# A joined graph kernel: one PSUM bank in four is emptied by VectorE in the SAGE stages, lists are loaded a step further ahead, and the node phase writes the first table itself

## The reference

```python
x = _layernorm(x + _L0_gnn_ref(x, ...))          # attention; its LayerNorm is the "node phase" below
def _sage_conv(x, src, dst, Wl, Wr, b):
    agg = segment_sum(x[src], dst) / maximum(cnt, 1)[:, None]
    return agg @ Wl.T + x @ Wr.T + b
h = relu(_bn_eval(_sage_conv(x, ...), ...))
h = _bn_eval(_sage_conv(h, ...), ...)
x = _layernorm(x + h)
```

## Time and profile before

| what | us |
|---|---|
| median of 3 runs | 10389.19 |
| lowest, highest | 10364.29, 10482.84 |
| the profiled execution | 10510.41 |
| its span in the trace | 10508.6 |
| TensorE, VectorE, ScalarE, POOL recorded busy | 6286.0, 4845.1, 3259.5, 5222.7 |
| mean granted TensorE clock | 0.667 |

### The profile page before, as it was taken

One profiled execution on the slowest core, in us unless ns is written; L12 is line 12 of the kernel. 1 busy time (PEld: TensorE's weight loads), 2 busy tenths in 40 slices (PEclk: granted clock), 3 DMA queues, 4 the chain that ended last, 5 costly groups with the idle time before them and its releaser, 6 DMA issues.

```text
span 10508.6 us, 188490 instructions
## 1 busy us (share of the span) xinstructions
PE 6286.0 (60%) x45410; PEld 4168.3 (40%) x45411; DVE 4845.1 (46%) x14741; ACT 3259.5 (31%) x7648; POOL 5222.7 (50%) x4883
## 2 busy tenths in 40 slices
PE   2255555455555754444444444446399999599999
PEld 2143434344343543444444444434244444244444
DVE  4344444444445315555555555541155555344454
ACT  0001010010102004333333444442155555355555
POOL 1365655556551005555555555514366666466665
PEclk9866666666666555555555555555599998788898
DMA  2322222122223332222122122212244433333333
GB/s 81 31 44 56 44 57 43 43 57 44 56 43 90 114 52 37 36 37 36 36 36 36 36 36 37 37 19 61 70 104 105 104 104 103 89 98 95 98 101 90
DMA packets 742656, 655.51 MB, mean 62 GB/s; under 512 B 455893, under 2 KB 635506, under 8 KB 742253
## 3 DMA queue, kind: packets, MB, share of 16 engines
q0 software_dynamic: 194624, 386.92, 17.2%
q1 hardware_dynamic: 476344, 244.24, 9.0%
q10 hardware_dynamic: 71640, 23.81, 0.9%
HBM read 570.87 MB, written 83.23 MB: 62 GB/s over the span
## 4 chain that ended last, share of the span: by engine, by line
PE 32%; issue 20%; another core or an unknown queue 14%; DVE 13%; DVEq 6%; ACT 5%; DMA 4%; SPq 3%; POOL 2%; ACTq 1%; POOLq 0%
PE psc L1387 10%; PE psa L1370 9%; PE psc L1257 2%; PE psa L1524 2%; PE psa L1296 2%; SPq L855 2%; ACT oht L1018 1%; ACT acc L1124 1%; DVEq L529 1%; ACT ohb L1015 1%; PE psc L1284 1%; DMA t_gat<-acc 1%; PE psc L1358 1%; PE psc L1360 1%
## 5 line engine op out<-in xcount | busy, mean ns | idle before, releaser
L552 POOL DMA_INDIRECT rows<-t_gat,idx x3200 | 3156.4, 986 | 2897.7 <-PE psa L1296 1149.7
L573 POOL DMA_INDIRECT acc<-t_part,acc x1400 | 1793.8, 1281 | 1036.4 <-issue 791.8
L1124 ACT ACTIVATE acc<-psa 128x384 bf16<-128x384 f32 x3200 | 1443.7, 497 | 1429.7 <-PE psa L1370 1163.4
L1296 PE MATMUL psa<-rhs,rows 128*128 128x176 f32 (+1 forms) x6400 | 1719.8, 422 | 152.2 <-issue 119.1
L1296 PEld LDWEIGHTS psa<-rhs,rows 128*128 128x128 f32 x6400 | 1492.7, 307 | 208.2 <-issue 177.3
L1370 PE MATMUL psa<-den,rhs 125*32 125x384 bf16 x12800 | 1189.6, 363 | 198.8 <-ACT acc L1124 149.3
L1018 ACT ACTIVATE oht<-psc 66x1024 bf16<-66x1024 bf16 x406 | 413.8, 1019 | 2295.2 <-remote 1912.3
L1387 PE MATMUL psc<-acc,oh_dst 128*125 128x384 bf16 x2300 | 851.1, 419 | 0.0
L1268 PE MATMUL psc<-adw,oht 66*128 66x17 bf16 (+1 forms) x3248 | 152.2, 173 | 1054.5 <-ACT oht L1018 1035.5
L1387 PE MATMUL psc<-acc,stg 128*125 128x384 bf16 x2300 | 743.4, 366 | 2.5 <-DMA acc<-t_part,acc 2.5
L1284 PE MATMUL psc<-oh,wgt 128*8 128x22 f32 (+1 forms) x6400 | 329.0, 206 | 678.7 <-issue 483.5
(11 more groups left out here) (321 smaller groups left out, 8261.2 us busy)
## 6 DMA issues: line engine op xcount, KB each, us to landing
rows<-list_src SPq DMA_DIRECT2D x200, 500.0 KB
rows<-t_gat,idx POOLq DMA_INDIRECT x3200
acc<-y_d SPq DMA_DIRECT2D x50, 1000.0 KB, 5.0
y_d<-stg SPq DMA_DIRECT2D x100, 250.0 KB, 2.0
acc<-t_part,acc POOLq DMA_INDIRECT x1400
acc<-t_sage SPq DMA_DIRECT2D x300, 62.5 KB
adw<-win_d SPq DMA_DIRECT2D x836, 2.2 KB
adw<-win_d SPq DMA_DIRECT2D x788, 0.4 KB
```

Source lines behind the costliest of these rows:

```text
L552: eng.indirect_dma_start(rows[:, j, 0:spec["width"]], None, spec["table"], bass.IndirectOffsetOnAxis(ap=idx[:, j:j + 1], axis=0)).then_inc ...
L573: eng.indirect_dma_start(h_prow[u][:, t, :], None, t_parts[layer], bass.IndirectOffsetOnAxis(ap=h_idx[u][:, t:t + 1], axis=0)).then_inc(h_ ...
L1124: eng.activation(h_rows[:, g, :], psa[:, g % 4, 0:D3], ACT.Copy).then_inc(hyb["ev"], 1)
L1296: last = eng.matmul(sums(half, q, h), rows[:, half * TH + j, 0:D], right, start=(j == 2 * q), stop=(j == 2 * q + 1))
```

## The change

In the SAGE node stages VectorE evicts the gathers 3, 7, 11 and 15, ScalarE the other twelve, with a semaphore each (`evd`, `ev`). TensorE's order becomes four segments, then four gathers, and so on. VectorE's order within a step is new. SP loads source and target list of tile t+1 in step t, where it loaded those of tile t; indices and own rows stay (`rest`, `own`). In the node phase VectorE applies factor and shift and makes the three parts, POOL only stores, and the parts of the first 16 chunks are written into `table1` in place of a buffer, so that the first layer's four loads of it go.

```diff
@@ -102,6 +102,20 @@
+def by_four_from_table(eng, in_table, *stages):
+    for lo, hi, table in ((0, in_table, True), (in_table, NC // 4, False)):
+        with eng.Fori(lo, hi) as i:
+            for first in (0, 2):
+                for stage in stages:
+                    for u in (first, first + 1):
+                        stage(i * 4, u, table)
+    for first in range(0, NC % 4, 2):
+        for stage in stages:
+            for u in range(first, min(first + 2, NC % 4)):
+                stage(NC // 4 * 4, u, False)
@@ -325,6 +339,9 @@
+        def fin_parts(e, u, table):
+            return table1[:, ds((e + u) * TC, TC), :] if table else z_parts[u % 2]
@@ -408,12 +425,11 @@
-        hyb = phase_sems("h", ("ohs", "ohd", "gps", "ev", "seg", "comb", "var", "std", "norm", "own"),
+        hyb = phase_sems("h", ("evd", "ohs", "ohd", "gps", "ev", "seg", "comb", "var", "std", "norm", "own"),
...
-        pool_l = sem("pool_l")
@@ -590,36 +606,23 @@
-        def pool_fin(eng, npl):
+        def pool_fin(eng):
...
-            def store(e, u):
-                link = DynLinks(eng, pool_l, npl)
-                z, parts = zt[:, u % 2, :, :], z_parts[u % 2]
+            def store(e, u, table):
...
-                eng.sem_inc(alone, 1)
-                eng.dma_start(rows_of(t_sage0, e + u), z).then_inc(S[f"out{u % 2}"], 16)
-                left = z
-                for r in range(3):
-                    link(eng.tensor_copy(parts[:, :, r * D:(r + 1) * D], left))
-                    eng.sem_inc(alone, 1)
-                    if r < 2:
-                        link(eng.tensor_tensor(z_rest, left, parts[:, :, r * D:(r + 1) * D], ALU.subtract))
-                        eng.sem_inc(alone, 1)
-                        left = z_rest
-                link.end()
-                eng.dma_start(rows_of(t_parts[0][AHEAD:, :], e + u), parts).then_inc(S[f"out{u % 2}"], 16)
-            def stored(e, u):
+                eng.dma_start(rows_of(t_sage0, e + u), zt[:, u % 2, :, :]).then_inc(S[f"out{u % 2}"], 16)
+                eng.dma_start(rows_of(t_parts[0][AHEAD:, :], e + u), fin_parts(e, u, table)).then_inc(S[f"out{u % 2}"], 16)
+            def stored(e, u, table):
...
-            by_four(eng, store, stored)
+            by_four_from_table(eng, KB // (4 * TC), store, stored)
-            ni, nk, fst, npl = (eng.alloc_register(f"{n}_pool") for n in ("ni", "nk", "fst", "npl"))
-            eng.reg_mov(npl, 0)
+            ni, nk, fst = (eng.alloc_register(f"{n}_pool") for n in ("ni", "nk", "fst"))
@@ -805,7 +808,10 @@
-                if before:
+            def rest(e, k):
+                u, n = k % 2, e + n0
+                if later(e, k):
@@ -819,10 +825,13 @@
             def step(e, t):
+                if there(e, t + 1):
+                    lists(e, t + 1)
...
-                    lists(e, t)
+                    rest(e, t)
...
+            lists(0, 0)
@@ -933,7 +942,7 @@
-                for k in range(0, KB, KB // 4):
+                for k in range(0, KB, KB // 4) if layer else ():
@@ -1090,13 +1099,6 @@
-            def finish(e, u):
-                eng.wait_ge(S["norm"], e + (u + 1))
-                for t in range(TC):
-                    z = zt[:, u % 2, t, :]
-                    last = eng.activation(z, z, ACT.Identity, bias=lnb[:, u % 2, t:t + 1], scale=lnr[:, u % 2, t:t + 1])
-                last.then_inc(S["row"], 1)
@@ -1105,10 +1107,10 @@
             def pair(stages, e, chunks):
-                pair([deviation, finish], i * 2, (0, 1))
+                pair([deviation], i * 2, (0, 1))
...
-            pair([deviation, finish], NC // 2 * 2 - 2, (0, 1))
-            pair([deviation, finish], NC - 1, range(NC % 2))
+            pair([deviation], NC // 2 * 2 - 2, (0, 1))
+            pair([deviation], NC - 1, range(NC % 2))
@@ -1141,11 +1143,11 @@
             def step(e, t):
-                    if gather:
+                    if gather and g % 4 < 3:
...
-                    if node and g == 5:
+                    if node and g == 7:
...
-                    if node and layer and g == 12:
+                    if node and layer and g == GP - 1:
@@ -1360,12 +1362,19 @@
+            def emptied(e, k, g):
+                k, g = (k - 1, g + GP) if g < 0 else (k, g)
+                if g % 4 == 3:
+                    eng.wait_ge(hyb["evd"], (e + n0) * 4 + (k * 4 + g // 4 + 1))
+                else:
+                    eng.wait_ge(hyb["ev"], (e + n0) * 12 + (k * 12 + g // 4 * 3 + g % 4 + 1))
             def gather(e, k, g):
-                    eng.wait_ge(hyb["ev"], n * GP + (k * GP + g - 3))
+                    emptied(e, k, g - 4)
@@ -1380,7 +1389,7 @@
-                    eng.wait_ge(hyb["ev"], n * GP + (k * GP + g + 1))
+                    emptied(e, k, g)
@@ -1389,15 +1398,17 @@
             def step(e, t):
-                for g in range(GT):
-                    if there(e, t - 1):
+                for first in range(0, GP, 4):
+                    for g in range(first, first + 4) if there(e, t - 1) else ():
...
-                    if there(e, t) and g < GP:
+                    for g in range(first, first + 4) if there(e, t) else ():
...
-                    if there(e, t - 2) and g == 4:
+                    if there(e, t - 2) and first == 4:
...
-                    if there(e, t - 2) and g == 10:
+                    if there(e, t - 2) and first == 8:
...
+                for g in range(GP, GT) if there(e, t - 1) else ():
+                    segment(e, t - 1, g)
@@ -1871,19 +1882,31 @@
+            def evict(e, k, g):
+                eng.wait_ge(hyb["gps"], (e + n0) * GP + (k * GP + g + 1))
+                eng.tensor_copy(h_rows[:, g, :], psa[:, g % 4, 0:D3]).then_inc(hyb["evd"], 1)
+
             def step(e, t):
                 if there(e, t):
-                    targets(e, t)
+                    evict(e, t, 3)
+                if there(e, t + 1):
+                    sources(e, t + 1)
+                if there(e, t):
+                    evict(e, t, 7)
                 if there(e, t - 2):
                     turned(e, t - 2)
-                if there(e, t + 1):
-                    sources(e, t + 1)
+                if there(e, t):
+                    evict(e, t, 11)
                 if there(e, t - 2):
                     centre(e, t - 2)
                     if layer:
                         scale(e, t - 2)
+                if there(e, t):
+                    evict(e, t, 15)
                 if there(e, t - 1):
                     combine(e, t - 1)
+                if there(e, t):
+                    targets(e, t)
@@ -2188,14 +2211,25 @@
-                def scale(e, u):
-                    own = Links(eng, S["own_b"], (e + u) * 2)
+                def scale(e, u, table):
+                    own = Links(eng, S["own_b"], (e + u) * 8)
...
-                    eng.sem_inc(S["norm"], 1)
-                by_four(eng, centre, scale)
+                    for t in range(TC):
+                        z = zt[:, u % 2, t, :]
+                        last = ts(z, z, lnr[:, u % 2, t:t + 1], lnb[:, u % 2, t:t + 1], ALU.mult, ALU.add)
+                    own(last)
+                    left = zt[:, u % 2, :, :]
+                    for r in range(PARTS):
+                        part_r = fin_parts(e, u, table)[:, :, r * D:(r + 1) * D]
+                        own(eng.tensor_copy(part_r, left))
+                        if r < PARTS - 1:
+                            own(tt(z_rest, left, part_r, ALU.subtract))
+                            left = z_rest
+                    eng.sem_inc(S["row"], 1)
+                by_four_from_table(eng, KB // (4 * TC), lambda e, u, table: centre(e, u), scale)
```

More of the change, by code:

```diff
@@ L688, in _ @@
             phase_end(eng, 7)
-            pool_fin(eng, npl)
+            pool_fin(eng)
             phase_end(eng, 8)
```

## The result

| kernel | median us | lowest, highest | executions |
|---|---|---|---|
| before | 10436.01 | 10364.29, 10501.15 | 4 |
| changed | 11807.43 | 11790.81, 11814.90 | 4 |

Ratio 1.131, 95% interval 1.122 to 1.141: slower, as forecast, but by 1371 us where 500 were forecast, and above the range, which ended at 11,650. The runs were made in sets, each with the kernel before beside it, and the kernel before took about 10,500 us (medians of 10,436 to 10,536) in some sets, this one among them, and about 8,900 in others, so ratios are taken inside a set, and a step is named with the set's condition, "10,500" or "8,900".

What follows compares the result with a forecast made beforehand. TensorE, not eviction, was taken to set the SAGE pace. Steps of 13.9 + 2.6 + 0.9 = 17.4 us gave +660 us, less 104 and 57: +499, so 10,890 us; range 10,200 to 11,650.

Steps and rivals of the forecast that it cites:

- The handover: SAGE step: TensorE's first segment waits for the mask, now behind `combine` on VectorE; 5.0 us a step.
- TensorE's batched step: SAGE step: TensorE's work with segments and gathers in batches, at full clock, takes 8.9 us, 2.9 less.
- The clock: SAGE step: after each stop TensorE restarts at 1.2 GHz, 5.2 us of work at half rate; +2.6 us a step.
- rival B: SAGE stages: clock stays at half through every step's work; 21.1 us a step, 11,630 us in all; chance 0.18.
- Late signals: SAGE step: VectorE waits five times for TensorE signals that come late; +0.9 us a step, bounds 0 and 2.5.
- Node phase: Node phase before SAGE: conversions moved from POOL to VectorE shorten two chunks from 28.2 to 19.9 us; -104 us.
- The table load: Before the first SAGE layer: without four loads on SP's queue, the index list and everything after come earlier; -57 us.
- A: SAGE stages: clock holds or returns at once; 13.9 to 14.0 us a step, 10,200 us in all; chance 0.15.
- C: SAGE stages: eviction is the bound and two engines halve it; step 12.0 us or below, 9810 us; chance 0.05.

Runs made afterwards that it cites:

- run 4: Changed kernel unaltered, measured again in a set where the kernel before took 8901.18 us: 9778.09 us, ratio 1.099, step 17.0 us.
- run 1: Changed kernel with only `targets(t)` moved back to the head of VectorE's step: 9183.22 us, ratio 1.030 to the kernel before.
- run 7: Kernel before with only `targets(t)` moved last in VectorE's step, behind `combine(t-1)`: 11476.47 us, ratio 1.289, step 25.0 us.
- run 6: Changed kernel with 26 extra matmuls, never read, at the end of each TensorE step: 9293.94 us, ratio 1.044, step 14.5 us.
- run 9: Beside the kernel before at 10,523 us: changed kernel unaltered, 11966.15 us; changed kernel with one of POOL's seven gathers per tile, 10972.62 us.
- run 10: Changed kernel with ScalarE emptying all 16 banks and VectorE's order of before, batches and lists kept: 8701.84 us, ratio 0.978, step 11.57 us.
- run 11: Two edits of run 10's kernel: one POOL gather per tile, 8355.09 us; target mask made by 23 small comparisons, 8531.30 us, ratio 0.958.
- run 12: Kernel before with the change's node phase, table load and lists a step ahead: 8722.24 us, ratio 0.980; in condition 10,500, 10401.41 us, ratio 0.989.

## Why the prediction was right or wrong

**The handover was right in place and near in size.** 5.0 us forecast; 5.21 in the step above, and on the mean 5.9 in the changed kernel and 5.75 in run 4, where no signal is late (total us, times, longest; the changed kernel, then run 4):

```profile
PE psc L1396 <- DVEq L1828: 1172.3, 200, 11.0
```
```profile
PE psc L1396 <- DVEq L1828: 1145.2, 199, 6.1
```

The terms of run 4, means against the forecast: `combine` begins 0.67 us behind the last segment's record (0.35; VectorE is often still evicting bank 15) and takes 1.20 with its gaps (0.95), small operation and gap 0.40 (0.42), mask 3.16 (3.15), signal 0.34 (0.1). With `targets` first the stop is gone (run 1); with it last in the kernel before it appears (run 7, 5.26).

**TensorE's batched step, 8.9 us, was right.** Run 6 shows 8.84 at full clock, and 8.84 + 5.75 + 2.4 gives the 17.0 measured without late signals.

**The clock, +2.6 us, was right:** 2.4 by run 6. That the forecast chose it over rival B was in part luck: nothing in the argument told the orders apart, the reason given was the time from rest at the layers' starts of the interleaved order, and with the handover the interleaved order went B's way (run 7).

**Late signals, +0.9 us, is the term that failed.** It was bounded at 0 to 2.5 by one lateness read in one step of the kernel before. Measured: 21.6 - 17.0 = 4.6 us between the conditions, and 4.8 by run 9. The trace of before held more than the step that was read: 228 evictions over 1 us late, up to 4.6 us, and a gather of POOL ran or had just ended in each of these delays. What it couldn't show is how much the interleaved order hid; that order loses only 1.9 us a step to the condition (14.0 against 12.05). In the changed kernel four gathers go out together, TensorE needs their banks some two microseconds later, and each stop costs clock as well. Inside a step, from the first segment to the last, TensorE takes 15.8 us on the mean where it takes 11.3 in run 4: 3.0 of the difference are stops, the other 1.5 longer busy time at the lower clock. The step is 4.2 us above the 17.4 forecast, or some 830 of the 871 us missed: late signals 3.7 more than priced and the handover 0.75 more, batches and clock 0.2 less.

**Node phase, -104 us, gave 57.** The period of two chunks fell from 28.2 to 24.2 us, forecast 19.9. The chain in the changed kernel:

```profile
7122.22 0.18 DVE L2217 RECIPROCAL lnr<-lnr 125x4 f32<-125x4 f32 x1
...
7127.07 0.18 DVE L2217 RECIPROCAL lnr<-lnr 125x4 f32<-125x4 f32 x1
...
7127.48 1.69 DVE L2222 TENSOR_SCALAR acc<-acc,lnr,lnb 125x128 f32<-125x128 f32 x4
...
7131.90 0.43 DVE L2227 CAST den<-rows 125x512 f32 x1
...
7134.47 1.32 POOL L616 DMA_DIRECT2D t_part<-den  x1
...
7143.86 0.69 DVE L2202 TENSOR_TENSOR acc<-psa,acc 125x512 f32<-125x512 f32 x1 [3.36 <-POOLq L620]
```

Scaling takes 4.9 and 5.3 us (7122.22 to 7127.07 to 7132.3) where 4.2 each was priced: the casts and subtractions had their price, the gaps between dependent operations and the second chunk's four scalings at 0.42 had not. From the last issue's end, 7135.8, to the `centre` that waits for it pass 8.1 us, not 5.6. The casts were right (0.43). **The table load, -57, gave 53.**

**Rivals.** A fell: the granted clock was 0.69, and even with the clock held by force (run 6) the step is 14.5 us. C, eviction as the bound, fell: splitting it costs 2.4 us (run 10), and ScalarE alone keeps up with 9.9 us (run 11). The rule that C cites from the Trainium skill ("TensorEngine Tiling (Array Packing)", section "PSUM Bottleneck") is for kernels that the PSUM copy may bound; here it didn't, as the earlier trace rows suggested, and sharing the copy lost time.

**Open.** What makes the condition in which signals are late isn't shown; it isn't tied to a chip, since one gave both, and it costs the untouched phases ahead some 1,200 us too (run 9), of which nothing was taken apart. Whether the changed kernel would lose less if SP loaded the index list ahead of the target list, so that POOL's gathers fell elsewhere in the step, wasn't run. Whether the signals alone or TensorE's work is held is argued only: gathers 10 to 12 and the products, recorded over more than 4 us, were released together near 8470.5.

A version that beats both kernels in both conditions, if by 1 to 2%, is run 12's: node phase, table and lists of the change, eviction and orders of before, ratios 0.980 and 0.989. Run 11's small masks reach 0.958 where signals aren't late, and weren't tried in the other condition.

## What to carry to other kernels

Before moving an operation to the end of an in-order engine's step, ask who wants its result first in the next one: behind an operation that waits for the consumer's last work it becomes a serial handover, and the stop costs clock on top. Price a signal's delay by what overlaps it and by how much slack the new order leaves, not by one delay that the old order showed. When a resource is no bound (here eviction), moving part of it to a loaded engine wins nothing and can add waits.

## What the runs showed of the hardware

- What waits for TensorE can begin 4 to 6 us behind its records, 1.43 us apart, while POOL issues indirect gathers. With the same program that happens in one condition (570 evictions of 3,200 over 1 us late, the latest 6.2) and not in the other (none over 0.6): 21.6 and 17.0 us a step.
- A two-tensor comparison of 128x2875 on VectorE holds an indirect gather of POOL to 2.7 to 3.8 us instead of 0.95 (run 10); 23 one-tensor comparisons of together 3.98 us don't hold it (run 11). The Trainium skill, "SBUF — State Buffer", section "Who interferes with whom", says that an operation with two SBUF inputs contends with GpSimd's reads, and infers that descriptor generation for transfers isn't stopped by it. The trace agrees with the first, as an indirect gather reads its row numbers from SBUF. It shows that the whole issuing of such a gather can be held; whether the reading or the making of descriptors is what waits, and so whether the second holds, no run here tells apart.
- After a stop of 5 us TensorE's granted clock was 0.50 (1.2 GHz) for 4 us of batched work and then 1.00 (the changed kernel, 8457.5 to 8468.3); in the interleaved order pairs still took the 0.95 us of the low clock 14 us after the stop (run 7).
